# Batch 2's second attention earlier in the last phase, and the halves of batch 4 first on every engine in the tail

## The reference

```
x = x + xattn0(ln(x), ctx)     # 16 heads of 8: softmax(q k^T * scale) v, then a projection
x = x + ffn0(ln(x))            # square(relu(x Ws1)) Ws2, plus experts whose weight trunc() makes 0 unless it is 1
x = x + xattn1(ln(x), ctx)     # one head of 128: softmax(q k^T) v
x = x + ffn1(ln(x))            # 8 experts: each takes its 256 most probable tokens of softmax(x Ws + bs)
```

## Time and profile before

| what | before |
|---|---|
| median of 3 runs | 211.41 us |
| the profiled execution | 210.27 us |
| its span, first to last instruction | 208.5 us |
| PE, DVE, POOL, ACT busy | 184.3, 130.9, 103.9, 90.3 us |
| mean granted clock of TensorE | 0.992 |
| last phase begins, tail begins | about 85 and 111 us |
| first scan of the search | 133.0 us |
| first gather | 149.65 us |

### The profile page before, as it was taken

How to read it: one execution, slowest core, us unless ns; L and a number is a source line. 1 busy time by engine, 2 the same in 40 slices (tenths; PEclk the granted TensorE clock), 3 DMA queues, 4 the chain that set the end, 5 groups by cost and what they waited for, 6 DMA issues and landing times.

```text
span 208.5 us, 3666 instructions
## 1 busy us (share of the span) xinstructions
PE 184.3 (88%) x1261; PEld 111.9 (54%) x1261; DVE 130.9 (63%) x453; ACT 90.3 (43%) x219; POOL 103.9 (50%) x115
## 2 busy tenths in 40 slices
PE   6988999997899989999999999799789978987960
PEld 2643543264434546376776766333378766776840
DVE  5698887566566779586699788898841823112210
ACT  2414772285322574146633562367764322333220
POOL 0599730952053021811147478500278888788742
PEclk9999999999999999999999999999999999999996
DMA  5725222201100001069910112100023233332323
GB/s 169 213 73 136 80 54 53 51 5 44 49 13 0 0 0 53 2 238 338 285 56 0 53 55 104 53 0 0 3 57 39 39 44 50 39 39 39 37 23 31
DMA packets 16127, 13.64 MB, mean 65 GB/s; under 512 B 3699, under 2 KB 13079, under 8 KB 16103
## 3 DMA queue, kind: packets, MB, share of 16 engines
q1 hardware_dynamic: 12246, 10.62, 16.9%
q0 software_dynamic: 2944, 2.30, 8.5%
q10 hardware_dynamic: 913, 0.43, 0.8%
HBM read 8.03 MB, written 3.21 MB: 54 GB/s over the span
## 4 chain that ended last, share of the span: by engine, by line
PE 52%; DVE 17%; POOL 11%; issue 9%; DMA 6%; ACT 2%; POOLq 1%; ACTq 0%; DVEq 0%
POOL out L2001 8%; PE psum L1041 7%; PE psum L1011 4%; PE psum L938 3%; DMA out<-pT,idx 3%; DVE pT L1716 3%; PE psum L948 3%; PE psum L1059 3%; PE psum L982 3%; PE psum L1013 3%; DVE mrow L1563 2%; POOL pT L1993 2%; DVE stats L1445 2%; PE psum L964 2%; PE psum L1387 2%
## 5 line engine op out<-in xcount | busy, mean ns | idle before, releaser
L1885 POOL TENSOR_SCALAR ve<-mv 128x4 f32<-128x4 f32 (+1 forms) x19 | 4.4, 230 | 64.9 <-DVE mv L1448 64.7
L1563 DVE TENSOR_REDUCE mrow<-psum 128x8 bf16<-128x616 f32 x32 | 24.8, 792 | 11.2 <-PE psum L982 11.2
L801 ACT ACTIVATE pT<-psum 103x512 f32<-103x512 f32 (+1 forms) x36 | 21.2, 596 | 23.8 <-PE psum L1013 23.6
L2001 POOL DMA_INDIRECT out<-pT,idx x16 | 25.5, 1595 | 8.2 <-issue 4.0
L938 PE MATMUL psum<-c 128*128 128x512 bf16 x109 | 28.6, 379 | 0.0
L1993 POOL DMA_INDIRECT pT<-gather_rows,idx x16 | 16.9, 1057 | 21.1 <-DVE idx L1774 16.8
L1789 DVE SCALAR_TENSOR_TENSOR pT<-psum,pT 128x128 f32<-128x128 f32 x16 | 5.1, 347 | 25.7 <-PE psum L1401 25.7
L1387 PE MATMUL psum<-xinT,w 128*128 128x256 f32 (+1 forms) x80 | 16.5, 349 | 3.8 <-ACT xinT L883 3.8
L888 ACT ACTIVATE pT<-psum,b 128x256 f32<-128x256 f32 (+1 forms) x40 | 14.8, 431 | 7.6 <-PE psum L1387 7.6
L1401 PE MATMUL psum<-w,pT 128*128 128x128 f32 x128 | 17.3, 283 | 0.2 <-DVE flag L1795 0.2
L1401 PEld LDWEIGHTS psum<-w,pT 128*128 128x128 f32 x128 | 16.1, 191 | 1.2 <-DVE flag L1795 0.3
(11 more groups left out here) (201 smaller groups left out, 370.7 us busy)
## 6 DMA issues: line engine op xcount, KB each, us to landing
w<-in_L_ffn_W SPq DMA_DIRECT2D x16, 256.0 KB, 5.7
gather_rows<-xrow SPq DMA_DIRECT2D x4, 272.0 KB, 2.1
x<-in_x SPq DMA_DIRECT2D x4, 256.0 KB, 5.2
q_stack<-q_hi SPq DMA_DIRECT2D x32, 32.0 KB, 1.8
out<-res SPq DMA_DIRECT2D x4, 256.0 KB, 2.2
q_stack<-q_lo SPq DMA_DIRECT2D x24, 32.0 KB, 1.8
b_rows<-in_L_ffn_b SPq DMA_DIRECT2D x1, 512.0 KB, 3.9
pT<-gather_rows,idx POOLq DMA_INDIRECT x16, 2.7
```

The source lines that it names most:

```text
L801: nc.scalar.activation(pT[0:n, b % 2, s, :], ST_ps[s % 2][0:n, :], ACT.Exp).then_inc(exp_done, 1)
L1563: dve.tensor_reduce(mrow[:, b % 2, u // 2, h0:h0 + 2 * GH].rearrange("p (c h) -> p c h", c=2), psum[:, to:to + 2, 0:GK].rearrange("p c (h ...
L2001: nc.gpsimd.indirect_dma_start(flat, bass.IndirectOffsetOnAxis(idx[:, h, e:e + 1], 0), y[:, e, h, :], None, bounds_check=last_row, oob_is_ ...
```

## The change

It changes no arithmetic. Five things:

1. In the last phase the second attention of batch 2 takes earlier slots, by a new table `SECOND_SLOTS` (its entries for phase 2 are the slots of before). `scores1` moves ahead of the last third of batch 3's attention (`attend(2, 2)`) on PE, `weigh1` ahead of the second slot's exponential on ACT, `scale1` ahead of `normalise` on DVE. `scale2` and `share` of batch 2 both lie in the phase now; `share` was in the tail.
2. In the tail each engine's list is put in another order, most steps of the halves ahead of the last steps of batch 3. On ACT `weigh1` of batch 3 is cut in two, with `copy_T(1, ub)` between, and still signals once.
3. The repeated shares of the last batch get a buffer of their own (`last_rep`) and a semaphore of their own; DVE's wait for PE's reading of batch 3's shares is gone.
4. PE's fillers in the tail are 24 instead of 31, at other places.
5. POOL writes batch 2's rows in the phase, and batch 3's behind its `repeat_share`.

```diff
+SECOND_SLOTS = {"scale1": (5, 1), "weights1": (7, 4), "inverse1": (7, 5), "attend1": (8, 6), "turn3": (9, 7), "route1": (10, 8), "scale2": (11, 9), "share": (11, 11)}
...
+        last_rep = pT[:, 0, 11, :]
```

ACT, in the slots and in the tail:

```diff
+                    if ph == B - 1 and s == 1:
+                        weigh1(t, t, 0, J)
                     act.wait_ge(st_ps_done, b * CH + s + 1)
...
             hidden(B - 1, ua, a0, a1, aps)
-            weigh1(t, t, 0, J)
+            spread_out(1)
+            weigh1(t, t, 0, J // 2, False)
             copy_T(1, ub, bps[0], b0, b1_)
+            weigh1(t, t, J // 2, J)
+            hidden(B - 1, ub, b0, b1_, bps)
+            copy_T(2, ua, aps1, a0, a1)
             weights1_T(t, 0, J, tail2_ps)
-            copy_T(2, ua, aps1, a0, a1)
-            hidden(B - 1, ub, b0, b1_, bps)
-            spread_out(1)
-            copy_T(3, t, tail2_ps)
             copy_T(2, ub, bps1, b0, b1_)
             weigh1(B - 1, ua, a0, a1)
+            weights1_T(ua, a0, a1, aps1)
+            copy_T(3, t, tail2_ps)
             weigh1(B - 1, ub, b0, b1_)
-            share_exp(t, t, 0, J)
-            weights1_T(ua, a0, a1, aps1)
             weights1_T(ub, b0, b1_, bps1)
             copy_T(3, ua, aps1, a0, a1)
+            share_exp(t, t, 0, J)
             copy_T(3, ub, bps1, b0, b1_)
```

PE, the end of the tail:

```diff
             warm(4, 3)
             weights1_T(ua, a0, a1, aps1)
-            warm(2, 3)
-            weights1_T(ub, b0, b1_, bps1)
+            residual_T(3, t, t, tail2_ps)
             warm(1, 3)
             attend1(B - 1, ua, a0, a1, aps1)
+            route1(t, 0, J, tail2_ps)
+            weights1_T(ub, b0, b1_, bps1)
+            residual_T(3, B - 1, ua, aps1, a0, a1)
+            warm(1, 3)
             attend1(B - 1, ub, b0, b1_, bps1)
+            route1(ua, a0, a1, aps1)
+            warm(1, 3)
+            residual_T(3, B - 1, ub, bps1, b0, b1_)
             warm(2, 3)
-            residual_T(3, B - 1, ua, aps1, a0, a1)
-            warm(3, 3)
-            residual_T(3, B - 1, ub, bps1, b0, b1_)
-            route1(ua, a0, a1, aps1)
+            route1(ub, b0, b1_, bps1)
+            warm(5, 3)
             spreads(t, t, 0, J)
-            route1(ub, b0, b1_, bps1)
-            warm(4, 3)
             spreads(B - 1, ua, a0, a1)
```

DVE, in `share` and in the tail:

```diff
                 if t == B - 1:
-                    dve.wait_ge(spread_ps_done, B - 1)
...
                 add_projection(B - 1, ub, b0, b1_, bps)
+                add_shared(B - 1, ua, a0, a1, aps)
                 stats1(B - 1, ub, b0, b1_)
-                add_shared(B - 1, ua, a0, a1, aps)
                 stats2(B - 1, ua, a0, a1)
-                share(t - 1, t - 1, 0, J)
-                share_rows(t - 1, t - 1, 0, J)
                 inverse1(t, t, 0, J)
-                add_attention1(t, t, 0, J, tail2_ps)
                 add_shared(B - 1, ub, b0, b1_, bps)
                 stats2(B - 1, ub, b0, b1_)
+                scale1(B - 1, ua, a0, a1, aps1)
+                add_attention1(t, t, 0, J, tail2_ps)
+                scale1(B - 1, ub, b0, b1_, bps1)
                 stats3(t, t, 0, J)
-                scale1(B - 1, ua, a0, a1, aps1)
-                scale1(B - 1, ub, b0, b1_, bps1)
+                inverse1(B - 1, ua, a0, a1)
+                add_attention1(B - 1, ua, a0, a1, aps1)
+                stats3(B - 1, ua, a0, a1)
+                inverse1(B - 1, ub, b0, b1_)
+                add_attention1(B - 1, ub, b0, b1_, bps1)
+                stats3(B - 1, ub, b0, b1_)
                 scale2(t, t, 0, J, tail2_ps)
...
```

More of the change, by code:

```diff
@@ L765, in hidden, with weigh1 @@
                 nc.scalar.activation(hid2[:, cols], hid[:, cols], ACT.Square).then_inc(hid2_done, 1)
-            def weigh1(t, u, j0, j1):
+            def weigh1(t, u, j0, j1, last=True):
                 act.wait_ge(sub1_done, u + 1)
@@ L1180, in _ @@
                     t = ph - 1
+                    if ph == B - 1 and s == 1:
+                        scores1(ph - 2, ph - 2, 0, J, tail2_ps)
                     if t == 0 and s < GC:
@@ L1240, in _ @@
                                   stop=True).then_inc(once_ps_done, 1)
+                    if ph >= 2 and s == second_slot(ph, "weights1") and ph == B - 1:
+                        weights1_T(ph - 2, 0, J, tail2_ps)
                     if t >= 0 and s == step_slot(ph, "project"):
@@ L1251, in _ @@
                     t = ph - 2
[L1252 removed]
+                    if t >= 0 and ph < B - 1 and s == 1:
                         scores1(t, t, 0, J, tail2_ps)
[L1254 removed]
+                    if t >= 0 and ph < B - 1 and s == second_slot(ph, "weights1"):
                         weights1_T(t, 0, J, tail2_ps)
[L1256 removed]
+                    if t >= 0 and s == second_slot(ph, "attend1"):
                         attend1(t, t, 0, J, tail2_ps)
[L1258 removed]
+                    if t >= 0 and s == second_slot(ph, "turn3"):
                         residual_T(3, t, t, tail2_ps)
[L1260 removed]
+                    if t >= 0 and s == second_slot(ph, "route1"):
                         route1(t, 0, J, tail2_ps)
@@ L1280, in _ @@
             scores1(t, t, 0, J, tail2_ps)
-            warm(1, 3)
-            hidden(ua, a0, a1, aps)
-            warm(3, 3)
-            project(ub, b0, b1_, bps)
-            warm(1, 3)
-            shared(ua, a0, a1, aps)
-            warm(2, 3)
-            residual_T(1, B - 1, ub, bps[0], b0, b1_)
-            warm(2, 3)
-            weights1_T(t, 0, J, tail2_ps)
+            hidden(ua, a0, a1, aps)
+            warm(2, 3)
+            project(ub, b0, b1_, bps)
+            shared(ua, a0, a1, aps)
+            spreads(1, 1, 0, J)
+            warm(3, 3)
+            residual_T(1, B - 1, ub, bps[0], b0, b1_)
+            warm(1, 3)
             residual_T(2, B - 1, ua, aps1, a0, a1)
             hidden(ub, b0, b1_, bps)
-            warm(2, 3)
-            attend1(t, t, 0, J, tail2_ps)
-            scores1(B - 1, ua, a0, a1, aps1)
-            shared(ub, b0, b1_, bps)
-            spreads(1, 1, 0, J)
-            warm(2, 3)
-            residual_T(3, t, t, tail2_ps)
-            warm(2, 3)
+            warm(1, 3)
+            weights1_T(t, 0, J, tail2_ps)
+            warm(1, 3)
+            shared(ub, b0, b1_, bps)
+            scores1(B - 1, ua, a0, a1, aps1)
+            attend1(t, t, 0, J, tail2_ps)
             pe.wait_ge(spread_done, 2)
             residual_T(2, B - 1, ub, bps1, b0, b1_)
-            route1(t, 0, J, tail2_ps)
+            warm(2, 3)
             scores1(B - 1, ub, b0, b1_, bps1)
@@ L1631, in _ @@
                                     ln0_stats(3)
+                        if ph == B - 1 and s == second_slot(ph, "scale1"):
+                            scale1(ph - 2, ph - 2, 0, J, tail2_ps)
                         t = ph - 1
@@ L1964, in _ @@
                     ln_rstd(3, ph - 2, ph - 2)
+                if ph == B - 1:
+                    rows(1, 1)
                 if ph >= 1:
@@ L1968, in _ @@
                     rows(0, 0)
+                if ph == B - 1:
+                    repeat_share(1)
             (ua, a0, a1, _, _), (ub, b0, b1_, _, _) = units(B - 1)
```

69 lines of the change are left out of this document (32 added, 37 removed).

## The result

The change made the kernel **slower: 213.92 us median of 20 executions (211.24 to 216.5) against 211.86 (20 executions, 210.38 to 216.37) of the kernel before; ratio 1.0078, interval 1.005 to 1.0105**. Forecast were 210.6 us, and 212.2 at most. The ratio counts, of each kernel, only the executions within 1.5% of its fastest (13 of the 20 here), while medians are of all executions. The change was run twice more, each time beside the kernel before on one chip: 1.0054 (1.0015 to 1.0093) and 1.011 (1.0045 to 1.0176).

What follows compares the result with a forecast made beforehand. DVE's queue bounds the tail: start 110.0, 21.4 us without waits, then 1.2 and 0.2 give 132.8, or 131.9 with fewer gaps. Taking 132.2, 0.8 earlier than before, gives 211.41 - 0.8 = 210.6 us, range 208.9 to 212.2.

Steps and rivals of the forecast that it cites:

- the waits of the tail: DVE's waits before the search: 1.2 us for `shared(ub)` and 0.2 for `attend1`, added to 131.4.
- rival 4: Granted clock falls in PE's hole near 127 us, slowing at least two search rounds; 214 us or more, chance 0.05.
- The new break of PE: Last phase: PE waits about 0.6 us near 92 for the exponential behind `weigh1` on ACT.
- slower start: Last phase on PE: L1122 takes 1.16 us against 0.89; the 0.3 was to go with the old wait.
- DVE's start: Batch 4's first `add_projection` on DVE starts at 110.0 instead of 109.08, 0.95 us later.
- The hole for `shared(ub)`: Tail: DVE arrives at 117.2, the second half's shared expert ends on PE at 118.4; a wait of 1.2 us.
- `add_attention1` of the second half waits some 0.2: Tail: this DVE step waits some 0.2 us for its `attend1` on PE.
- The waits that go: Tail: DVE's waits for rstd (0.4 us) and exp (0.2 us) disappear.
- The gaps that are no waits: DVE's tail: 1.7 us of small gaps, of which 0 to 0.9 might go.
- Rival 2: The phase eats the gain: new break 1.2 us or more, search starts at 133; 211.4 us, chance 0.2.
- Rival 3: POOL's `rows` beside the search delay small DVE steps by 2.4 us, about 130 to 136; 213.0 us, chance 0.08.
- Warm-up matmuls: PE's tail fillers, 31 to 24: removing 7 counts nothing; at most 3.2 us if PE ended last.

Runs made afterwards that it cites:

- e14: The change itself, unaltered, run a third time beside its filled version; ratio to the kernel before 1.011 (1.0045 to 1.0176).
- e8: Phase of before with the change's tail, six more fillers in PE's hole, and batch 2's share, `spread_out(1)`, `scale2` and `spreads(1, 1)` moved; ratio to before 1.0001.
- e5: The change without the two fillers ahead of the last `route1`, PE idle 1.84 us instead of 1.41; ratio to the kernel before 1.0048.
- e6: The kernel before without the four fillers ahead of the last `spreads`, PE idle 1.91 us instead of 1.03; ratio to the kernel before 1.0138.
- e12: The kernel before with two of the four fillers ahead of the last `spreads` removed, PE idle 1.46 us; ratio to the kernel before 1.0108.
- e2: The change's tail alone, with the last phase of the kernel before and batch 2's `share` in the tail; ratio to the kernel before 1.0047.
- e7: The change with eight fillers instead of two ahead of the last `route1`, run a second time; ratio to the kernel before 1.0028.
- e4: The change with eight fillers instead of two ahead of the last `route1`, first run; ratio to the kernel before 0.9986.
- e11: As e8, with batch 2's share one step earlier on DVE and POOL's `repeat_share(1)` ahead of `ln_rstd(2, ua)`; ratio to the kernel before 0.9932.
- e13: The kernel before with eight fillers instead of four ahead of the last `spreads`, run a second time; ratio to the kernel before 0.9999.
- e10: The same program as e8, run again unaltered; ratio to the kernel before 0.9962 (0.9922 to 1.0002).

## Why the prediction was wrong

The forecast was 0.8 us faster, in the schedule; the schedule became 0.2 us slower, and most of the other 1.4 us (0.78% is 1.65) goes when PE's hole is filled: filled against open is 0.7 and 1.05%, against wider 0.2%. Two steps failed. In the sum it is the waits of the tail, taken as 1.2 + 0.2 and measured as 0.57 + 1.22 + 0.81 us. Beside the sum it is the clock, which it put at nothing on the strength of the earlier trace rows; that term, with a chance of 0.05 for rival 4, was the largest error. How much of the 1.4 us the slow matmuls themselves are is shown only for the search (0.6 us in e14).

- *The new break of PE.* Right: 0.64 us at 92.77, forecast 0.6 near 92. The old wait before `attend1` went, that of 0.24 before `route1` stayed. PE left the phase at 111.10, not 110.8: the 0.3 for a "slower start" of `attend1` was never there to win. It set a timeline's length (1.16) against a distance in the chain (0.89); L1122 in the tail, whose distance that is, has 1.06 in the timeline, and `attend1` of batch 2 takes 1.16 us after the change too. Before, in the tail:

```profile
117.16 1.06 PE L1122 MATMUL psum<-v,p1T 77*128 77x128 f32 x8
```

- *DVE's start.* 110.29, forecast 110.0. The sum was 0.25 short at `shared` of batch 3, which came at 106.36 instead of 106.1; this is that same 0.3.
- *The hole for `shared(ub)`.* Right in size, 1.22 against 1.2; but the 0.57 before it at `inverse1` was missed. By the order of the lists both come from `spread_out(1)` standing ahead of `weigh1` on ACT; I followed that chain to PE and not to DVE's own reader of `weigh1`. In e8, where `spread_out(1)` and `spreads(1)` stand later, the first is gone and the second is 0.37; the edits were not tried one by one.
- *"`add_attention1` of the second half waits some 0.2".* It waits 0.81. By the lists, `weights1_T(ub)` stands behind `route1` of batch 3 (1.06 us) on PE, and its `weigh1` on ACT behind the first half's weights and `copy_T(3)` of batch 3. e8's edit puts `scale2` into it, and 0.16 is left.
- *The waits that go* did go: none for POOL's rstd, none for ACT's exponential. The gaps that are no waits were 22.90 - 19.18 - 2.60 = 1.1 us, as taken. The search came at 133.19, forecast 132.2: 0.3 from the start and 1.2 from the two waits, less 0.5 for DVE's work, which is 19.18 and not 19.7.
- *Rival 2*, the phase eats the gain, came true in the schedule, though not by the break that it named: through DVE's later start.
- *Rival 3* is refuted. POOL's eight `rows` steps ran beside the last shares and the first scans, and none of them got longer by more than 0.01 us (compare):

```profile
L1914 POOL TENSOR_SCALAR xrow<-res,mv,rstd x16: 791/796/812, 85.7 to 136.4; 128x128 f32<-128x128 f32 x16
...
L1733 DVE TENSOR_SCALAR_CACHE_REDUCE pT<-pT,search_state x6: 1278/1279/1280, 133.2 to 143.6; 128x1024 bf16<-128x1024 f32 x6
...
L1551 DVE TENSOR_TENSOR xrow<-lg,lm x5: 163/191/243, 85.9 to 132.9; 128x32 f32<-128x32 f32 x3, 128x16 f32<-128x16 f32 x2
```

By the Trainium skill ("SBUF — State Buffer", "Who interferes with whom") the two-input steps of DVE should have waited for POOL's 0.8 us steps; the longest of L1551 is 0.243 us, and the measurement decides.
- *Rival 4*, the clock. I found the hole (1.5 us near 127 forecast, 1.41 before 129.58 found) and argued it away with the earlier trace rows, where the clock stood at 1.00 through 3.4 us without a matmul. That row stops just short of the answer. PE's last matmul ends near 201.6, and in the same trace the clock falls behind the row's end, 3.5 us into that idle stretch:

```profile
205.00:206.00 1.00, 0.00 (x0) 0.00 (x0) 0.00 (x0) 0.00 (x0) 0.00 (x0) 0.54 0.70 55
```

And a row of one execution could not say that a shorter hole is safe: in e14 the clock is 1.00 and 0.91 in the windows that hold the idle time and 0.50 in the one behind, where PE is busy 2.00 of 2.00. "Warm-up matmuls: removing 7 counts nothing while DVE is the queue" failed with it: PE is not on the path until its clock falls, then the search's fillers are. I had priced it at 1.5 us for each of two rounds; between first scan and first gather it costs 0.6 (e14) to 2.0 us (e5) where it happens.

The Trainium skill, "TensorE: Matmul & The Clock Gate", section "HAM oscillation — how this bites in real kernels", says that waits of PE bring it back to the lower clock, and the next piece of work starts slow. The traces of e5, e6, e12 and e14 agree, with 3.03 us in e12 instead of 1.89 for eight fillers, though the waits in its example are 3 to 5 us long and these 1.4 to 1.9. The trace of e2 does not: the clock fell there while PE was busy. That it takes only some executions of one program is seen in the change itself (full clock in the profile shown first, 0.50 in e14's).

## What to carry to other kernels

A filler matmul is priced not by the path of one quick execution but by the hole that it leaves when it goes: look for the longest idle stretch of PE that a reordering makes, above all ahead of work that must run at full clock, and fill it where it costs no step. When two orders differ by tenths of a microsecond, take several traces and compare milestone by milestone, since what differs in one trace may be any execution's. Where an idle stretch is to show that the clock holds, read on to the end of it. And after moving a step up in one engine's list, ask on every other engine which waiting instruction now has ready work behind it.

## What the runs showed that I had not expected

- Between 1.03 and 1.46 us of idle time in the same place of the same program lies the step from no loss to 1.1%. In the changed schedule 1.41 us costs 0.7 to 1.1% against filled, but 1.84 us on another chip only 0.2%: the length of the hole alone does not give the size. Over the 8 us ahead of the search PE is busy 6.21 us in the kernel before, 5.96 in the change and 7.25 filled; by that sum before and change hardly differ, and yet they behave differently. Windows of before, after, and e7:

```profile
125.01:129.01 4.00, 3.54 (x25) 2.45 (x25) 3.45 (x18) 1.35 (x5) 3.10 (x6) 1.00 0.20 78
129.01:133.01 4.00, 2.67 (x18) 1.53 (x17) 3.29 (x19) 0.58 (x3) 3.91 (x6) 1.00 0.15 57
```

```profile
125.19:129.19 4.00, 2.83 (x18) 1.63 (x17) 3.02 (x19) 0.80 (x4) 2.34 (x5) 1.00 0.00 0
129.19:133.19 4.00, 3.13 (x19) 1.98 (x20) 3.56 (x21) 0.84 (x5) 2.91 (x4) 1.00 0.00 0
```

```profile
125.06:129.06 4.00, 3.85 (x24) 2.21 (x22) 3.03 (x19) 0.80 (x4) 2.33 (x5) 1.00 0.02 4
129.06:133.06 4.00, 3.40 (x21) 1.98 (x20) 3.56 (x22) 0.84 (x5) 2.91 (x4) 1.00 0.00 0
```

- The clock also falls where no kernel here differs. PE stands idle for 1.36 us in each of the seventeen traces, near 51 us (54 in e14, which ran later); in e4, e11 and e13 the clock falls behind it, between 52 and 54 us, and their last phases start at 87.1 to 88.0 us instead of 85.4. In the other fourteen it stays at 1.00. This is the next place for a filler, which no run here tried. In e4:

```profile
52.01 0.30 PE L994 MATMUL psum<-k_max,q_hi 32*128 32x308 f16 x2 [1.36 <-DVE mrow L1580]
```

- The same program's stretch from first gather to last scatter took 53.6 or 55.6 us (e8, e10).
